# Another explicit order of all steps behind the first attention's loops, and predicated copies that wait themselves

## The reference

```python
# layer 0, attention: 2 sequences of 512, 16 heads of 128
q, k, v = causal_conv_silu(x @ W.T); q, k = l2norm(q), l2norm(k)
pred = k_t . state; delta = beta * (v_t - pred)
state = state + k_t (x) delta; o_t = q_t . state      # scan over 512 tokens
o = rms_norm(o) @ Wo.T
# layer 0, ffn: 8 experts of 176, 2 of them per token, and a shared MLP
# layer 1, attention: 2 sequences, 2 heads, chunks of 64 tokens, fast weights w0, w1, w2
gate = k @ w0; hb = k @ w2; hidden = silu(gate) * hb; dhidden = v @ w1.T
w1g = newtonschulz(hidden*lr1, v); w0g = newtonschulz(k*lr0, dgba); w2g = newtonschulz(k*lr2, dhbm)
w = normed(w + wg); o = silu(q @ w0) * (q @ w2) @ w1  # new weights; next chunk follows
# newtonschulz, 2 rounds: A = X X.T; B = b A + c A A; X = a X + B X
# layer 1, ffn: 6 experts of 176, 2 of them per batch of 512 rows, gelu; then the sum
```

## Time and profile before

| | |
|---|---|
| median of 3 runs | 1737.67 us (1737.56 to 1738.3) |
| span of the profiled execution | 1736.8 us, mean granted clock of TensorE 0.988 |
| TensorE busy | 1661.8 us (96%) |
| VectorE busy | 1466.0 us (84%) |
| ScalarE busy | 1202.0 us (69%) |
| GpSimd busy | 1101.6 us (63%) |

### The profile page before, as it was taken

One profiled execution on the slowest core, in us unless ns is written; L12 is line 12 of the kernel. 1 busy time (PEld: TensorE's weight loads), 2 busy tenths in 40 slices (PEclk: granted clock), 3 DMA queues, 4 the chain that ended last, 5 costly groups with the idle time before them and its releaser, 6 DMA issues.

```text
span 1736.8 us, 41710 instructions
## 1 busy us (share of the span) xinstructions
PE 1661.8 (96%) x14092; PEld 1223.9 (70%) x14092; DVE 1466.0 (84%) x3682; ACT 1202.0 (69%) x2912; POOL 1101.6 (63%) x1149
## 2 busy tenths in 40 slices
PE   8999899999999999999999999999997689999989
PEld 5577567777777777777777777777765566777677
DVE  5322599999999999999999999999985799999963
ACT  2134477777777877777777777777763488888863
POOL 1700167777777777776666666666665678888851
PEclk9999999999999999999999999999998799999999
DMA  9433310110110101100001010000002000000023
GB/s 316 165 104 106 101 32 23 38 32 27 31 37 21 40 21 37 31 24 25 27 16 30 15 28 24 18 24 27 15 9 61 1 1 2 1 2 2 1 77 107
DMA packets 66114, 73.85 MB, mean 43 GB/s; under 512 B 10991, under 2 KB 54783, under 8 KB 65791
## 3 DMA queue, kind: packets, MB, share of 16 engines
q1 hardware_dynamic: 62935, 63.92, 12.7%
q0 software_dynamic: 3072, 8.65, 1.5%
HBM read 55.45 MB, written 17.10 MB: 42 GB/s over the span
## 4 chain that ended last, share of the span: by engine, by line
PE 81%; DVE 8%; ACT 4%; POOL 3%; issue 2%; DMA 1%; SPq 0%; DVEq 0%; POOLq 0%
PE banks L786 20%; PE banks L945 7%; PE banks L813 4%; PE banks L900 3%; PE banks L919 3%; PE banks L821 3%; PE banks L829 3%; PE banks L858 3%; PE banks L751 3%; PE banks L866 3%; PE banks L872 2%; PE banks L1080 2%; PE banks L865 2%; PE banks L1001 2%; PE banks L770 2%
## 5 line engine op out<-in xcount | busy, mean ns | idle before, releaser
L786 PE MATMUL banks<-xnT,hw 128*128 128x512 f32 x768 | 414.1, 622 | 2.5 <-DVE cv L2099 2.5
L2155 DVE CAST_PREDICATED MM<-lmask,banks 128x512 bf16<-128x512 uint32 x384 | 272.3, 709 | 39.3 <-PE banks L866 33.3
L2099 DVE SCALAR_TENSOR_TENSOR cv<-banks,hc,cv 128x510 f32<-128x510 f32 (+2 forms) x384 | 284.6, 741 | 5.5 <-ACT cv L1500 0.8
L1564 ACT ACTIVATE T<-banks 128x256 bf16<-128x256 f32 x384 | 148.7, 387 | 154.2 <-PE banks L858 154.2
L2766 POOL TENSOR_TENSOR X<-X,yrow 128x512 f32<-128x512 f32 x128 | 163.3, 1277 | 67.9 <-ACT yrow L1596 67.9
L2730 POOL TENSOR_TENSOR kn<-nsum,half_pos 128x4 f32<-128x4 f32 x64 | 65.5, 1023 | 141.9 <-DVE nsum L2124 141.9
L866 PEld LDWEIGHTS banks<-MM,T 128*128 128x128 bf16 x1536 | 103.9, 98 | 64.2 <-issue 47.3
L865 PEld LDWEIGHTS banks<-T,MM 128*128 128x128 bf16 x1280 | 98.6, 97 | 66.4 <-ACT T L1564 64.8
L2099 DVE SCALAR_TENSOR_TENSOR cv<-banks,hcv,cv 128x510 f32<-128x510 f32 (+2 forms) x192 | 141.3, 736 | 1.4 <-ACT cv L1500 1.3
L858 PEld LDWEIGHTS banks<-MM,Gb 128*128 128x128 bf16 x1536 | 83.9, 98 | 82.7 <-issue 43.7
L945 PE MATMUL banks<-ho,OT 128*128 128x256 f32 x512 | 142.2, 401 | 0.0
(11 more groups left out here) (319 smaller groups left out, 4870.8 us busy)
## 6 DMA issues: line engine op xcount, KB each, us to landing
MM<-in_eye SPq DMA_DIRECT2D x64, 256.0 KB, 2.7
slot_rows<-zeros SPq DMA_DIRECT2D x1, 5304.0 KB, 21.1
slot_out<-ye SPq DMA_DIRECT2D x13, 384.0 KB, 2.7
xs<-slot_rows SPq DMA_DIRECT2D x12, 408.0 KB, 4.0
hw<-in_hw SPq DMA_DIRECT2D x16, 256.0 KB, 3.4
wT<-in_winit SPq DMA_DIRECT2D x8, 384.0 KB, 4.4
wgu<-in_wgu SPq DMA_DIRECT2D x1, 2816.0 KB
w1c<-in_ew SPq DMA_DIRECT2D x16, 176.0 KB
```

The lines of the kernel that those rows point to most:

```text
L786: ins = pe.matmul(PROJ[t][:], hw[:, kk, t, :], xnT[:, kk, u.b * BLK:(u.b + 1) * BLK], start=(kk == 0), stop=(kk == KD - 1))
L1564: act.activation(strips(T1[:].rearrange("p i t -> p (i t)"), LEVELS[lv], 0, 1), grams_bank(u)[:, 0:TILES * 64].rearrange("p (k e) -> p k e ...
L2099: dve.scalar_tensor_tensor(o, y, taps_of(t)[:, TAPS - 1 - i:TAPS - i], o, ALU.mult, ALU.add).then_inc(dve_conv, 1)
L2155: dve.copy_predicated(dst, m, ps).then_inc(dve_mm, 1)
```

## The change

On TensorE, ScalarE, VectorE and GpSimd everything behind the loops stands in one explicit list for each engine, with names x0 to x15; `pair_period`, `pair_units` and `STAGES` are gone. The steps are the same, each as often as before, but for one: ScalarE runs `gate_exponentials()` twice, first behind `silu_gate(x1)` (it stood behind `keep_total(x0)`), and again between `keep_v(x5)` and `silu_queries(x2)`. In VectorE's `invert` the increment ahead of the copy is gone, in the loops too, so that the copy has the waits itself.

The order differs nearly everywhere, and from period to period. Among the differences: `mask(a63)` on GpSimd stands behind `weight_roots()` (before: just ahead of `rhs_minus(a63, 1, 1)`), `rate_hidden(x0)` behind `add_rows(a63, 1)` (before: ahead of `add_squares(a63)`), `rates_begin(2)` ahead of `norm_stats(3, 1)`. On TensorE `turn_qk(x1)` and `turn_v(x1)` stand ahead of `second_turn(3, 0)`, `project_qk(x2)` too. Between `grads(x, 0)` and `grads(x, 1)` stood `newton(·, 0, 0, NEXT)` and `newton(·, 1, 1, GRAM)` in every period; now these are, for x4, NEXT, `output(x1)` and `newton(x2, 1, 1, SQUARE)`, for x8 NEXT and `project_v(x9)`, for x12 the same as before, for others one of such mixtures. In the tail `turn_output(x12)` comes behind `newton(x13, 1, 1, NEXT)`, `up(0)` ahead of `newton(x14, 1, 0, SQUARE)`, `up(3)` ahead of `newton(x15, 1, 0, TURN)`.

The diff, cut: the copies, a part of the passage on TensorE, ScalarE's two calls, and the tail on TensorE.

```diff
                 dve.wait_ge(pe_inv, 13 * u.n + 2 * lv + 1)
                 if lv == 0:
                     dve.wait_ge(w_eye[u.b], 16 * u.h + 16)
-                dve.sem_inc(waited, 1)
                 dst = both_strips(u.b, size)
                 m = lmask[:, lv].unsqueeze(2).to_broadcast([P, 2, TILES, 64])
                 ps = grams_bank(u)[:].rearrange("p (a k e) -> p a k e", a=2, e=size)
...
-            turn_qk(x1)
             rate_logits(3)
-            turn_v(x1)
             gates(x1)
+            project_v(x2)
             hidden_back(x1)
-            project_qk(x2)
             newton(x0, 0, 0, TURN)
             newton(x0, 0, 0, GRAM)
             newton(x0, 0, 0, SQUARE)
             grads(x1, 0)
-            for n in range(3, STEPS):
-                pair_period(n)
+            newton(x0, 0, 0, NEXT)
+            grads(x1, 1)
+            newton(x0, 0, 1, TURN)
+            turn_qk(x2)
+            newton(x0, 0, 1, GRAM)
+            turn_v(x2)
+            project_qk(x3)
+            newton(x0, 0, 1, SQUARE)
+            total(x1)
+            gates(x2)
+            newton(x0, 0, 1, NEXT)
+            project_v(x3)
+            hidden_back(x2)
+            newton(x0, 1, 0, TURN)
+            newton(x0, 1, 0, GRAM)
+            newton(x1, 0, 0, TURN)
+            newton(x0, 1, 0, SQUARE)
+            newton(x0, 1, 0, NEXT)
+            newton(x1, 0, 0, GRAM)
+            newton(x0, 1, 1, TURN)
+            newton(x1, 0, 0, SQUARE)
+            newton(x0, 1, 1, GRAM)
+            grads(x2, 0)
...
+            keep_v(x1)
+            silu_qk(x2)
+            square_qk(x2)
             keep_total(x0)
-            gate_exponentials()
-            keep_v(x1)
             keep_hidden(x1)
             half_tanh(x1)
-            silu_qk(x2)
             silu_gate(x1)
+            gate_exponentials()
             newton(x0, 0, 0, TURN)
-            square_qk(x2)
...
+            keep_weight(x2, 1)
+            keep_turned(x1)
+            keep_v(x5)
+            gate_exponentials()
+            silu_queries(x2)
+            newton(x3, 1, 0, TURN)
...
             gate_queries(x13)
             newton(x14, 1, 0, TURN)
             newton(x14, 1, 0, GRAM)
+            newton(x15, 0, 0, TURN)
+            up(0)
             newton(x14, 1, 0, SQUARE)
-            newton(x15, 0, 0, TURN)
+            newton(x15, 0, 0, GRAM)
+            turn_weight(x13, 2)
             newton(x14, 1, 0, NEXT)
-            spread_weights()
-            newton(x15, 0, 0, GRAM)
-            newton(x14, 1, 1, TURN)
-            turn_weight(x13, 2)
             turn_mixed(x13)
             newton(x15, 0, 0, SQUARE)
-            output(x13)
+            newton(x14, 1, 1, TURN)
+            newton(x15, 0, 0, NEXT)
             newton(x14, 1, 1, GRAM)
-            up(0)
+            turn_weight(x14, 0)
             newton(x14, 1, 1, SQUARE)
-            newton(x15, 0, 0, NEXT)
-            turn_output(x13)
-            newton(x14, 1, 1, NEXT)
-            turn_weight(x14, 0)
             newton(x15, 0, 1, TURN)
             turn_weight(x14, 1)
+            output(x13)
+            newton(x15, 0, 1, GRAM)
             up(1)
-            newton(x15, 0, 1, GRAM)
...
```

More of the change, by code:

```diff
@@ new lines, in _ @@
+            project_qk(x9)
+            output(x5)
+            newton(x7, 0, 0, SQUARE)
+            newton(x6, 1, 1, TURN)
+            grads(x8, 0)
+            newton(x7, 0, 0, NEXT)
+            project_v(x9)
+            grads(x8, 1)
+            newton(x7, 0, 1, TURN)
+            turn_qk(x9)
+            newton(x6, 1, 1, GRAM)
+            newton(x7, 0, 1, GRAM)
+            turn_weight(x6, 0)
+            newton(x6, 1, 1, SQUARE)
+            total(x8)
+            newton(x7, 0, 1, SQUARE)
@@ new lines, in _ @@
+            total(x9)
+            newton(x8, 0, 1, SQUARE)
+            turn_qk(x10)
+            turn_output(x6)
+            gate_queries(x7)
+            newton(x8, 0, 1, NEXT)
+            turn_v(x10)
+            project_rows(x6)
+            turn_mixed(x7)
+            newton(x8, 1, 0, TURN)
+            gates(x10)
+            hidden_back(x10)
+            newton(x8, 1, 0, GRAM)
+            turn_weight(x7, 2)
+            newton(x9, 0, 0, TURN)
+            newton(x8, 1, 0, SQUARE)
+            output(x7)
@@ new lines, in _ @@
+            turn_weight(x9, 0)
+            total(x11)
+            newton(x10, 0, 1, SQUARE)
+            turn_weight(x9, 1)
+            turn_qk(x12)
+            newton(x10, 0, 1, NEXT)
+            turn_output(x8)
+            turn_v(x12)
+            gate_queries(x9)
+            gates(x12)
+            newton(x10, 1, 0, TURN)
+            hidden_back(x12)
+            newton(x10, 1, 0, GRAM)
+            turn_weight(x9, 2)
+            newton(x11, 0, 0, TURN)
+            newton(x10, 1, 0, SQUARE)
@@ new lines, in _ @@
+            turn_mixed(x9)
+            project_qk(x13)
+            newton(x11, 0, 0, GRAM)
+            newton(x10, 1, 0, NEXT)
+            output(x9)
+            newton(x10, 1, 1, TURN)
+            newton(x11, 0, 0, SQUARE)
+            grads(x12, 0)
+            newton(x11, 0, 0, NEXT)
+            newton(x10, 1, 1, GRAM)
+            grads(x12, 1)
+            newton(x10, 1, 1, SQUARE)
+            newton(x11, 0, 1, TURN)
+            project_v(x13)
+            newton(x10, 1, 1, NEXT)
@@ new lines, in _ @@
+            turn_weight(x11, 0)
+            newton(x12, 0, 1, GRAM)
+            project_v(x14)
+            total(x13)
+            newton(x12, 0, 1, SQUARE)
+            turn_qk(x14)
+            turn_weight(x11, 1)
+            turn_v(x14)
+            newton(x12, 0, 1, NEXT)
+            gates(x14)
+            turn_output(x10)
+            newton(x12, 1, 0, TURN)
+            gate_queries(x11)
+            newton(x12, 1, 0, GRAM)
+            hidden_back(x14)
+            newton(x13, 0, 0, TURN)
@@ L1343, in _ @@
[L1343 to L1352 removed]
+            grads(x14, 1)
+            newton(x12, 1, 1, NEXT)
+            output(x11)
+            newton(x13, 0, 1, GRAM)
+            project_v(x15)
+            turn_weight(x12, 0)
@@ L1435, in _ @@
             output(x15)
+            up(7)
+            turn_output(x15)
             down(5)
-            turn_output(x15)
-            up(7)
             down(6)
```

1672 lines of the change are left out of this document (1454 added, 218 removed).

## The result

The changed kernel takes 1742.26 us (median of 13 runs, 1740.1 to 1743.93) against 1737.79 us (13 runs) for the kernel before: ratio 1.0021, 95% interval 1.0014 to 1.0029. The forecast was 1729.4 us, 1716 to 1741; the sign and the range were both wrong. The profiled execution has a span of 1741.0 us, 4.2 more than that of before. The 13 executions fall into two groups: seven with a mean granted clock of 0.984 or 0.985 took 1742.3 to 1743.9 us, the profiled one among them, and six with 0.988 took 1740.1 to 1741.2.

A forecast was written before the change was run, and what follows sets the result against it. TensorE, busy 1661.8 of 1736.8 us, was taken as the bound, so only its idle time could go. Terms -0.5 - 6.3 + 1.5 - 3.0 + 0 = -8.3 gave a 1728.5 us span, 1729.4 as median; range 1716 to 1741.

The forecast's parts named there:

- VectorE's copies: Copies that wait themselves: gain hidden by TensorE's work in the loops, 0.5 us won behind them, 0.8 at most.
- the copies pay in the loops as well: Rival: TensorE's 100% busy share may hide waits in the loops; up to 12.5 us more won, 1717 us; chance 0.06.
- The reading of 0.38 against 0.19 us: VectorE's mean idle ahead of copies against self-waiting additions in the loops; the 0.19 difference was a carried wait's maximum cost.
- The steady periods: The 13 second-attention periods: work stays, idle time goes, 0.5 us each; 6.3 us won, ends 0 and 12.8.
- So the 0.35 goes: In each period, TensorE's 0.35 us wait ahead of grads(·,1) for ScalarE's gradient copy vanishes under longer cover.
- The second gate_exponentials: Two table loads, a Silu and an Exp on ScalarE near x5, 3.0 us; 1.5 us lost, ends 0 and 3.0.
- The passage: From the loops' end to the periods: 3 us won, 1.2 by the earlier mask, about 1.8 by ScalarE; ends -8, +2.
- The tail: Last stretch with the ups: full work in another order ends at the same time, 0; ends -4.2 and +3.8 us.
- The stall of 1 us: In the tail, TensorE waits 1 us or so for the weights of up(3).
- the win that I set against it: In the tail, covered Newton waits of x14 and x15 win about as much as the 1 us stall.
- The slower one: Rival: late second-round weights make the next pair wait, 0.45 to 0.8 us a period; 1741.6 to 1746 us; chance 0.15.
- The unshrunk period: Rival: VectorE's queue sets the period, so removing TensorE's wait only moves it; 1735.7 us, 1733 to 1739; chance 0.19.

The follow-up runs named there:

- copies_inc_back: New lists up to total(x2), then the old order, one gate_exponentials, but the increment ahead of VectorE's copies put back; 0.9981 of the kernel before.
- copies_only: The kernel before, old orders written out on every engine, with only VectorE's copies waiting themselves; 0.9996 of the kernel before.
- x1_first: New lists to total(x2), then old order, copies waiting themselves; x1's gradient steps moved ahead of rates_end(3) and the choice of experts; 0.9965 of the kernel before.
- periods_new: The changed kernel without its second gate_exponentials, and with the old order again from about total(x14) on; 1.0006 of the kernel before.
- no_second_exp: The changed kernel without its second gate_exponentials; 1.0002 of the kernel before.
- swapped_scale: copies_only with VectorE's weight_scale(x,1,0) put one place later, behind grad_norm, for x3 to x12; 1.0034 of the kernel before.
- unblocked: no_second_exp with 13 small VectorE steps moved to keep them from starting during GpSimd's additions; 1.0036 of the kernel before.
- new_tail: New lists to total(x2), old periods, copies waiting themselves, then the changed kernel's tail from about grads(x14,0); 0.9979 of the kernel before.

## Why the prediction was wrong

- *VectorE's copies, in the loops nothing, behind them -0.5.* The sign was right, the place wrong. The loops gave 1.5 us (copies_inc_back undoes it), though TensorE's busy share was 855.66 of 856 us; "100% busy" hid 0.02 us a unit and 0.5 us around the 50th. This is the rival that had 0.06 (the copies pay in the loops as well), with a small part of its 12.5 us. The reading of 0.38 against 0.19 us as the price of a carried wait fails: the waits that remain are still 0.38 us each, there are fewer. Behind the loops copies_only shows no gain, and one of 0.5 us could not be told there.
- *The steady periods, -6.3.* This is the step that failed, in its term for VectorE: "The same steps stand in both orders, so work stays (TensorE 17.3 us a period, VectorE 17.5)". The other half, "So the 0.35 goes", came true (3.5 us of waits in ten periods became 0.4) and was worth nothing. I took the work of VectorE as fixed and its 1.02 us of idle time as the limit both ways. But the length of its steps depends on what GpSimd does at that moment: the old order has the small steps just ahead of GpSimd's additions, in the new one ten of them in twelve periods are held. The new periods lose 4.1 to 4.2 us (periods_new, no_second_exp), while VectorE's steps grow by 4.4 us and its idle time stays; swapped_scale shows that one such step a period costs 0.94 us a period. That the longer steps are all of the 4.2 us is argued from this, not shown: the trial to take them away (unblocked) only moved them.
- *The second gate_exponentials, +1.5.* In the old order exactly that (1.54). In the new order 3.5, over my upper end of 3.0; the 3.4 us at half clock behind the wait were in no term.
- *The passage, -3.* -5.0, within the ends, but not by the sum: it won 9.4 us up to x0's first Newton turn (8.9 to 11.4 in the other kernels with this passage and these copies) and lost about half again by total(x3). One knot there I had named (rates_end(3) and the choice ahead of x1's gradients) but priced at nothing; x1_first took it away and gained 2.1 us at total(x1), so it is at most a part. VectorE's steps are 5.4 us longer in the passage too, 1.8 of it in rates_end; no run tells what that costs. So the closeness to -3 is partly luck.
- *The tail, 0.* +4.8, beyond the upper end of 3.8. "Another order of full work ends at the same time" fails: the new order isn't full. By itself the new order costs 3 us in waits (new_tail: for weights, for VectorE's addition behind a long weighing, for a Newton step behind up(0)). In the changed kernel 10 us at half clock around up(0), which my sum did not have, take more: 4.3 us of longer matmuls, and only 1.4 us more idle time than in the old tail. The stall of 1 us that I had for up(3) was 1.3 us in new_tail; the win that I set against it did not come.
- *Sum.* -1.6 us (ahead of the first unit, where the code is the same but for the increment), -1.7, -5.0, +7.7 and +4.8 are the +4.2 us between the two profiled executions.
- *Rivals.* The slower one had 0.15, for weights of the second round that come late and make the next pair wait. The periods did decide, with 0.35 us a period and the table loads, and the tail with them. TensorE's waits in periods_new show no such lateness, so its sign came true and its mechanism did not. The unshrunk period (0.19) named VectorE's queue, which was right, but took its length as given.

The experiments point to a version that beats both kernels: the new lists up to total(x2), then the order of before, with copies that wait themselves and one gate_exponentials. It was timed on two chips, at 0.9950 and 0.9954 of the kernel before, some 8 us.

## What to carry to other kernels

When a dense hand-made order is exchanged, the durations in the profile of the old order are not constants: ask for each short VectorE step on SBUF which GpSimd instruction will be running when it starts, since here it was held for up to the whole length of that one. Cut a large reordering into stretches by the starts of steps that both kernels share; here one stretch won 5 us under a total that lost 4. And where the new order makes TensorE wait, its granted clock belongs into the sum: half speed behind a wait or under up(0) cost time that no wait shows, and the same passage took 3.7 us more in an execution with a lower clock.

## What the runs showed of the hardware

- VectorE steps of 0.16 us (128 x 4 with two SBUF operands, 128 x 2 with one) took up to 1.11 us (unblocked) and 0.75 us (the changed kernel) when a GpSimd addition over 128 x 512 of SBUF was running, and ended 0.01 to 0.03 us behind it. A VectorE step that started 0.02 us before the addition was not held (swapped_scale, the step of x12).
- A switch of ScalarE's table for one Exp and back takes 3.0 us on ScalarE; it cost 1.5 us in one order and 3.5 in another, there with 3.4 us of TensorE at half clock behind it.
- The same passage code took 145.8 us at a mean granted clock of 0.86 and 149.5 at 0.82.
- The kernel before took 1737.8 us on one chip and medians of 1753 to 1757 on others. In copies_only, which is the same code up to the loops but for the increment, the first square_sums started 18.7 us later than in the trace of before on the first chip, and the loops took no longer.
